# Two-layer attention and FFN kernel: the heads stage's loop over groups written out on four of five engines

## The chip, the cores and the metric

One core of a Trainium2 chip. The core has five engines that run their own instruction streams: TensorE (PE: matmuls, with weight loads shown apart as PEld), VectorE (DVE), ScalarE (ACT), GpSimd (POOL) and SyncE (SP, used here as the queue that issues transfers). They meet only through semaphores. The metric is the device time of one execution in microseconds, lower is better; the time given is the median of the runs.

## What is computed

Two layers, each an attention part and a feed-forward part with a residual, over x of 16 batches x 128 rows x 512 columns. The part that the change touches is the first layer's attention, an mLSTM with 16 heads of 32 columns, whose core is, cut from the reference:

```
log_D = log_fg + transpose(ig)              # gates, lower triangle only
D  = exp(log_D - max_log_D)
C  = einsum('bhsd,bhtd->bhst', qh, kh) / sqrt(dh) * D
normalizer = maximum(abs(C.sum(-1)), exp(-max_log_D))
h  = einsum('bhst,bhtd->bhsd', C / (normalizer + EPS), vh)
hn = (h - mu) * rsqrt(var + EPS) * ln_scale  # per head
x  = x + hn
```

Beside it the same stage computes the keys of the second layer's attention, `ctx @ ki_w + ki_b` (2048 rows x 512 by 512 x 2048), and the sum of their squares, since both read what is already in place.

## The kernel before

The kernel is a row of stages, each with its own block of code for each engine, with a barrier of all engines between stages. The stage of the change is `heads_and_keys`. It works in G = 4 groups of GB = 4 batches. A group has PER = 16 steps; step n stands for head n of the mLSTM and, LAG = 8 steps behind, for head m of the keys. What each engine does in one step:

- PE (L1178, `body`): `keys`, 12 matmuls of 128x512 in three passes (L100 to L102) for one head's keys; in each fourth step (n = 2, 6, 10, 14) `scores` for four heads at once (L1148); then `outputs`, four products of the decayed scores with the values (L1160). `keys` waits for `wt_done` (DVE) and for `ksq_done` of the key two steps earlier (ACT, L944), because the keys use two banks in turn.
- ACT (L950, `body`): in even steps `pair` copies two heads' results out of the bank (L902) and waits for `pv`, the count of PE's `outputs`; then `weight_lead` (L928), `exp` (L892, four calls), `keep_key` (L939, L944, and the transfer L948, which ACT's queue issues). In steps 4 and 5 two squares (L917) and in step 7 a square root (L921) for the group before.
- DVE (L1055): decayed scores (L1008), the weights' low part (L1043), the sum of squares (L1053), and the group before's mean, variance and row statistics.
- POOL (L843): masks (L794), copies of the values (L803), and four element-wise steps for the group before (L779, L820, L830, L839).
- SP (L709): issues all loads, each behind a wait for the buffer that it fills.

Nothing reorders the work: each engine's order is the order of the code above. Group 0 is written out for every engine (`body(0, True)`). Groups 1 to 3 are a hardware loop on each engine: `with act.Fori(1, G) as g` at L971, the same at L1077 (DVE), L864 (POOL) and L1187 (PE), and `sp.Fori(1, G - 1)` at L754, after which SP has its last group written out. In a loop the group number is a register, so that the places and the semaphore values that depend on it are computed by register instructions beside the work. A loop's end is a register add and a conditional branch back to its start; the first instruction behind a taken branch is the register instruction of the same line.

On DVE the helper `Own` counts instructions that wait for their own engine; `enter` and `leave` tell it about the loop.

A later stage, `attend_and_last`, has loops of the same kind for four engines at L2411 and for SP at L2479; the change doesn't touch them.

Of the kernel before, what the change touches and what calls it, by code (L numbers as in the profile page):

```python
# [29 lines left out]
G = B // GB  # L30
# [555 lines left out]
def heads_and_keys(nc, K, M, A, E1, ctx_dram, ln_scale, xn_dram, ct_dram, g_dram, split_dram, w_dram, b_dram, k_dram, rk):  # L586
# [11 lines left out]
    with Phase(nc, "heads") as ph:  # L598
# [72 lines left out]
        def _(sp):  # L671
# [79 lines left out]
            sp.wait_ge(qk, 4)  # L751
            load_q(0, 2)
            body(0, True)
            with sp.Fori(1, G - 1) as g:  # L754
                body(g, False)
            body(G - 1, False, True)
            for m in range(PER - LAG + 1, PER):
# [24 lines left out]
        def _(pool):  # L782
            pool.sem_inc(norm_done, FIRST)
            pool.sem_inc(res_done, FIRST)
            own = Own(pool, own_pool)
# [57 lines left out]
            def body(g, first):  # L843
                for n in range(PER):
                    mask(g, n + AHEAD)
                    if 5 <= n < 8:
                        for b in ((0,), (1, 2), (3,))[n - 5]:
                            value(after(g, PER)[0], g + 1, b)
                    if not first:
                        for at, step in ((3, centre), (8, scale), (10, weigh), (12, add)):  # L850
                            if at <= n < at + 2:
                                step(g - 1, 2 * (n - at))
                                step(g - 1, 2 * (n - at) + 1)
# [7 lines left out]
            nc.gpsimd.memset(total[:], 0.0).then_inc(total_blank, 1)  # L861
            pool.wait_ge(loaded_w, 16)
            body(0, True)
            with pool.Fori(1, G) as g:  # L864
                body(g, False)
            pool.wait_ge(E1.loaded, 48)
            pool.wait_ge(product, (G - 1) * PER)
# [14 lines left out]
        def _(act):  # L882
# [67 lines left out]
            def body(g, first):  # L950
                for n in range(PER):
                    if n % 2 == 0:
                        if n:
                            pair(g, n // 2 - 1)
                        elif not first:
                            pair(g - 1, PAIRS - 1)
                    lagging(g, n - LAG + 1, weight_lead)
                    exp(g, n + 2, first)
                    lagging(g, n - LAG - 1, keep_key)
                    if not first:  # L960
                        if n == 1:
                            row_sums(g - 1)
                        if n == 4 or n == 5:
                            square(g - 1, n - 4)
                        if n == 7:
                            deviation(g - 1)
# [1 line left out]
            exp(0, 0, True)  # L968
            exp(0, 1, True)
            body(0, True)  # L970
            with act.Fori(1, G) as g:  # L971
                body(g, False)
            last = G - 1
            pair(last, PAIRS - 1)
# [25 lines left out]
        def _(dve):  # L1000
            own = Own(dve, own_dve)
# [53 lines left out]
            def body(g, first):  # L1055
                for n in range(PER):
                    decayed(g, n + 1, first)
                    lagging(g, n - LAG + 1, weight_trail)
                    lagging(g, n - LAG - 1, add_square)
                    if not first:  # L1060
                        if n == 1:
                            divisor(g - 1)
                        if n == 1 or n == 2:
                            mean(g - 1, n - 1)
                        if n == 5 or n == 6:
                            variance(g - 1, n - 5)
                        if n == 7:
                            factor(g - 1)
                        if n >= PER - GB // 2:
                            if n == PER - GB // 2:  # L1070
                                dve.wait_ge(res_done, FIRST + g)
                            for b in range(2):
                                row_stats.batch((g - 1) * GB + 2 * (n - PER + GB // 2) + b)

            decayed(0, 0, True)
            body(0, True)
            with dve.Fori(1, G) as g:  # L1077
                own.enter(g - 1, 7)
                body(g, False)
            own.leave(G - 1)  # L1080
            last = G - 1

            def finish(m):
# [1825 lines left out]
```

## Time and profile before

| what | value |
|---|---|
| median of 3 runs | 1503.14 us (1502.87 to 1508.75) |
| the profiled execution, own time | 1506.08 us |
| its span, first to last instruction | 1504.3 us |
| granted TensorE clock, mean over the span | 0.942 of full speed |
| PE busy | 1372.5 us, 91% |
| ACT busy | 771.0 us, 51% |
| DVE busy | 825.4 us, 55% |
| POOL busy | 402.8 us, 27% |
| heads stage, about | 258 to 570 us of the span |

Times in a row are microseconds from the start of the span unless marked ns. A group of instructions has its line, its engine, what it writes and reads, how often it ran, and, in brackets, how long its engine sat idle before it and what it is held to have waited for. An engine's name with a q (ACTq) means its sequencer: register, branch, semaphore and transfer instructions, which don't count as busy. A granted clock of 1.00 means 2.4 GHz, of 0.50 means 1.2 GHz.

### The profile page before, as it was taken

To read this page: it belongs to the slowest core of one execution; us is meant where nothing else is said; L and a number is where in the kernel's file an instruction comes from. 1 tells how busy PE (TensorE), PEld (TensorE's weight loads), DVE (VectorE), ACT (ScalarE), POOL (GpSimd) and SP (SyncE) were. 2 spreads that over 40 slices of the span, in tenths; PEclk is the share of its full clock that TensorE was granted. 3 is DMA by queue.
4 is the path that set the end of the run, shared out by engine and by line. 5 is a ranking of instruction groups with operands and counts; after the bars stand their busy time and mean duration, and the time that the engine had idled before them with its cause. 6 is when DMAs were issued, how large, how long until landed. Compare 5 with 4: busy or idle time off the path is not lost. (4 is left out here: it accounts for less than half of the span.)

```text
span 1504.3 us, 25964 instructions
## 1 busy us (share of the span) xinstructions
PE 1372.5 (91%) x7406; PEld 1138.1 (76%) x7407; DVE 825.4 (55%) x1534; ACT 771.0 (51%) x1874; POOL 402.8 (27%) x375
## 2 busy tenths in 40 slices
PE   6899998999898987998999865999976999999998
PEld 5786666888787867876877644887866888888887
DVE  2432332367676786535444227744328877777866
ACT  4223222578686855215555543535447666666661
POOL 0110101427272810346943015211015500000032
PEclk9999999699999996998999996999987999999999
DMA  7998333887787730347564666654535555555412
GB/s 240 354 337 317 142 140 123 295 285 258 237 267 238 258 115 1 113 154 219 169 195 133 213 226 194 194 200 140 181 112 154 166 157 161 161 159 164 138 48 112
DMA packets 171909, 280.91 MB, mean 187 GB/s; under 512 B 29809, under 2 KB 64369, under 8 KB 171569
## 3 DMA queue, kind: packets, MB, share of 16 engines
q1 hardware_dynamic: 146976, 227.58, 47.6%
q0 software_dynamic: 7712, 26.22, 5.3%
q10 hardware_dynamic: 17136, 26.09, 4.7%
q8 instruction: 40, 0.66, 0.2%
q14 instruction: 45, 0.36, 0.1%
HBM read 173.14 MB, written 106.70 MB: 186 GB/s over the span
## 5 line engine op out<-in xcount | busy, mean ns | idle before, releaser
L2548 ACT ACTIVATE attend_prob<-banks,attend_row,rq 128x128 f32<-128x128 f32 x256 | 113.9, 455 | 53.6 <-DVE attend_row L2623 53.5
L100 PE MATMUL banks<-of_shared_split,heads_wl 128*128 (+1 forms) x256 | 109.6, 428 | 18.6 <-ACT heads_ksq L944 13.5
L100 PE MATMUL banks<-of_shared_split,of_ctx_lead 128*128 128x512 f32 x256 | 106.8, 417 | 9.3 <-DVE of_ctx_trail L419 5.5
L100 PE MATMUL banks<-attend_wol,attend_ol 128*128 (+1 forms) x256 | 105.9, 414 | 0.0
L100 PE MATMUL banks<-of_x_lead,queries_wl 128*128 128x512 f32 x256 | 102.0, 398 | 3.9 <-ACT queries_sq L2183 2.4
L101 PE MATMUL banks<-of_shared_split,heads_wl 128*128 (+1 forms) x256 | 103.8, 405 | 0.0
L102 PE MATMUL banks<-of_shared_split,heads_wt 128*128 (+1 forms) x256 | 103.7, 405 | 0.0
L101 PE MATMUL banks<-of_shared_split,of_ctx_lead 128*128 128x512 f32 x256 | 103.4, 404 | 0.0
L102 PE MATMUL banks<-of_shared_split,of_ctx_trail 128*128 128x512 f32 x256 | 103.2, 403 | 0.0
L101 PE MATMUL banks<-of_x_trail,queries_wl 128*128 128x512 f32 x256 | 101.1, 395 | 0.0
L102 PE MATMUL banks<-of_x_lead,queries_wt 128*128 128x512 f32 x256 | 100.8, 394 | 0.0
L102 PE MATMUL banks<-attend_wol,attend_ot 128*128 (+1 forms) x256 | 100.6, 393 | 0.0
L101 PE MATMUL banks<-attend_wot,attend_ol 128*128 (+1 forms) x256 | 99.7, 389 | 0.0
L2179 ACT ACTIVATE queries_head<-banks,queries_bias 128x512 f32<-128x512 f32 x64 | 44.2, 690 | 95.9 <-PE banks L102 83.8
L1053 DVE TENSOR_TENSOR heads_total<-heads_total,heads_ksq 128x512 f32 (+1 forms) x64 | 62.6, 978 | 53.6 <-ACT heads_ksq L944 53.3
L2255 DVE TENSOR_TENSOR queries_total<-queries_total,queries_sq 128x512 f32<-128x512 f32 x60 | 41.7, 695 | 91.5 <-ACT queries_sq L2183 91.4
L892 ACT ACTIVATE heads_dec<-mlstm_gmax,mlstm_nat 128x128 f32<-128x128 f32 x264 | 83.3, 388 | 5.9 <-POOL mlstm_gmax L794 5.9
L2530 POOL TENSOR_TENSOR x_kept<-x_kept,attend_tern_bias 128x512 f32<-128x512 f32 x12 | 15.5, 1295 | 264.3 <-ACT of_attend_raw L2586 262.7
L2561 ACT ACTIVATE attend_ol<-banks,of_attend_vbias 128x512 fp32r<-128x512 f32 x64 | 44.1, 689 | 70.3 <-PE banks L2753 70.2
L2647 DVE TENSOR_TENSOR x_kept<-x_kept,banks 128x512 f32 (+1 forms) x64 | 44.0, 687 | 62.8 <-PE banks L102 62.2
L1160 PEld LDWEIGHTS banks<-heads_ctx,heads_cmat 128*128 128x128 f32 x512 | 71.6, 209 | 8.6 <-POOL heads_ctx L803 3.1
L2734 PE MATMUL banks<-attend_kn,attend_q 128*128 128x128 f32 x512 | 71.4, 285 | 5.5 <-DMA attend_q<-q_heads 5.5
(339 smaller groups left out, 3612.1 us busy)
## 6 DMA issues: line engine op xcount, KB each, us to landing
mlstm_gmax<-running_max SPq DMA_DIRECT2D x36, 512.0 KB, 5.9
heads_raw<-in_L_xattn_ki_w SPq DMA_DIRECT2D x32, 512.0 KB, 6.3
k_heads<-heads_key ACTq DMA_DIRECT2D x64, 256.0 KB, 4.6
q_heads<-queries_head SPq DMA_DIRECT2D x64, 256.0 KB, 2.4
attend_q<-q_heads SPq DMA_DIRECT2D x64, 256.0 KB, 4.1
of_attend_k<-k_heads SPq DMA_DIRECT2D x60, 256.0 KB, 4.0
of_attend_v<-v_heads SPq DMA_DIRECT2D x60, 256.0 KB, 3.3
sorted_rows<-values_zeros SPq DMA_DIRECT2D x2, 5120.0 KB, 18.1
```

The lines of the kernel that those rows point to most:

```text
L100: nc.tensor.matmul(out, lead_l, lead_r, start=first, stop=False)
L101: nc.tensor.matmul(out, lead_l, trail_r, start=False, stop=False)
L102: return nc.tensor.matmul(out, trail_l, lead_r, start=False, stop=last)
L892: ins = nc.scalar.activation(dec[:, n % 2, b], gmax[:, h // 2 % 4, h % 2 * N + b * S:h % 2 * N + (b + 1) * S], ACT.Exp, scale=-1.0, bias=M ...
L1053: nc.vector.tensor_tensor(t, t, ksq[:, m % 2, :], ALU.add).then_inc(total_done, 1)
L1160: ins = nc.tensor.matmul(ps[:, n // 2 % 2, at:at + DH0 + 1], cmat[:, n % RING, b, :], ctx1[:, bass.ds(half(g), 1), b, n, :].rearrange("p a ...
L2179: nc.scalar.activation(head[:, u % HEADS_RING, :], ps[:, u % 4, :], ACT.Identity, bias=bias[:, h:h + 1]).then_inc(head_done, 1)
L2255: nc.vector.tensor_tensor(t, t, sq[:, u % 2, :], ALU.add).then_inc(total_done, 1)
L2548: ins = nc.scalar.activation(prob[:, j % 2, b, :], ps[:, j % 2, b * S:(b + 1) * S], ACT.Exp, bias=row[:, j % 2, 1, b:b + 1], scale=rq[:, b ...
L2561: nc.scalar.activation(ol[:, par, j, :], ps[:, 4 + j % 2, :], ACT.Identity, bias=vbias[:, bass.ds(quad_of(it) * 4 + j, 1)]).then_inc(ol_do ...
L2647: nc.vector.tensor_tensor(xb, xb, ps[:, 6 + b % 2, :], ALU.add).then_inc(acc_done, 1)
L2734: ins = nc.tensor.matmul(ps[:, j % 2, s], q[:, j, s], kn[:, j % 2, s], start=True, stop=True)
```

## The change

The loops over groups 1 to 3 of ACT, DVE and POOL, and over groups 1 and 2 of SP, become Python loops: the body is written out once for each group, with the group number known when the code is made. PE keeps its hardware loop. `Own` on DVE needs no word about a loop any more.

```
@@ SP, L751 @@
             sp.wait_ge(qk, 4)
             load_q(0, 2)
             body(0, True)
-            with sp.Fori(1, G - 1) as g:
+            for g in range(1, G - 1):
                 body(g, False)
             body(G - 1, False, True)
@@ POOL, L861 @@
             body(0, True)
-            with pool.Fori(1, G) as g:
+            for g in range(1, G):
                 body(g, False)
@@ ACT, L968 @@
             body(0, True)
-            with act.Fori(1, G) as g:
+            for g in range(1, G):
                 body(g, False)
@@ DVE, L1074 @@
             body(0, True)
-            with dve.Fori(1, G) as g:
-                own.enter(g - 1, 7)
+            for g in range(1, G):
                 body(g, False)
-            own.leave(G - 1)
```

Two things follow from the group number being known. The register instructions of these four engines go away. And conditions in the code that ask `isinstance(g, int)` now take the other side; one of them changes a wait (`value`, L797, below).

In the rows that follow, a semaphore that this stage took over from an earlier one stands under its old name: `values_first_loaded0` is `pv`, `values_ct_stored3` and `values_xT_stored` are `raw_loaded`, `values_wt_done` is `product`, `values_x_loaded1` and `values_x_loaded3` are `masked` and `c_done`, `values_product` is `key_done`, `values_cleared` is `total_done`, `values_g_stored` and `values_turned` are `key_stored`. ISA and REGISTER_ALU are register instructions.

ACT, before: the end of step 15 and of the loop's body; behind the branch comes the body's start (L902) again.

```order
L892 ISA
L892 ACTIVATE heads_dec<-mlstm_gmax,mlstm_nat 128x128
L937 ISA [waits values_wt_done]
L939 ACTIVATE heads_key<-banks,heads_kbias 128x512 [waits values_g_stored]
L944 ACTIVATE heads_ksq<-banks,heads_kbias 128x512 [waits values_cleared]
L948 ISA [waits values_product]
L948 DMA k_heads<-heads_key 128x512
L971 REGISTER_ALU
L971 COMPARE_AND_BRANCH
```

ACT, after: the same place, the end of step 15 of group 1 and the start of step 0 of group 2.

```order
L892 ACTIVATE heads_dec<-mlstm_gmax,mlstm_nat 128x128 x3
L939 ACTIVATE heads_key<-banks,heads_kbias 128x512 [waits values_wt_done,values_g_stored]
L944 ACTIVATE heads_ksq<-banks,heads_kbias 128x512 [waits values_cleared]
L948 DMA k_heads<-heads_key 128x512 [waits values_product]
L902 ACTIVATE heads_hraw<-banks 128x4x66 [waits values_first_loaded0]
L928 ACTIVATE heads_wl<-heads_raw 128x512 [waits values_ct_stored3,values_wt_done]
```

The copy of the last pair (L902) now stands directly behind the transfer's issue; the register instruction ahead of each L892, ahead of L939 and ahead of L948 is gone, and no instruction with work in it has another place.

POOL, before: step 5 of the loop's body, where the next group's values are copied; the wait for `pv` stands in each group.

```order
L794 AFFINE_SELECT mlstm_gmax<-mlstm_gmax 128x512 [waits mlstm_g_ring1]
L799 ISA
L801 REGISTER_ALU [waits mlstm_loaded_ctx]
L803 REGISTER_ALU [waits values_first_loaded0]
L803 REGISTER_ALU x2
L803 ISA
```

POOL, after: the same step in group 3, the last.

```order
L794 AFFINE_SELECT mlstm_gmax<-mlstm_gmax 128x512 [waits mlstm_g_ring1]
L803 COPY heads_ctx<-mlstm_ctx 128x16x32 [waits mlstm_loaded_ctx]
L794 AFFINE_SELECT mlstm_gmax<-mlstm_gmax 128x512 [waits mlstm_g_ring1]
L803 COPY heads_ctx<-mlstm_ctx 128x16x32 x2
```

In group 3 the copy for a fifth group (which doesn't exist; the code fills it with group 0's values again) no longer waits for `pv`; in groups 1 and 2 it still does. The order of PE's instructions is the same before and after.

## Rows read from the trace of the kernel before

**Rows 1.** Windows, busy us by engine (count), granted clock, DMA share, GB/s.

```profile
320.07:388.00 67.93, 65.88 (x449) 55.56 (x448) 49.94 (x63) 52.62 (x120) 36.81 (x36) 0.97 0.79 265
388.00:460.31 72.31, 66.14 (x450) 55.75 (x448) 48.90 (x64) 54.67 (x126) 37.86 (x36) 0.95 0.77 249
320.07:323.83 3.76, 3.76 (x22) 3.22 (x20) 1.89 (x3) 3.54 (x9) 0.64 (x1) 1.00 0.99 368
388.00:397.90 9.90, 5.67 (x21) 4.57 (x20) 3.97 (x8) 6.49 (x16) 0.64 (x1) 0.66 0.73 225
460.31:469.64 9.33, 5.40 (x22) 4.36 (x20) 3.60 (x7) 6.49 (x16) 0.64 (x1) 0.82 0.69 227
323.83:329.32 5.49, 5.12 (x54) 4.13 (x52) 4.64 (x9) 4.54 (x11) 0.00 (x0) 1.00 0.79 286
397.90:402.97 5.07, 5.07 (x55) 4.13 (x53) 3.22 (x5) 3.30 (x9) 0.00 (x0) 1.00 0.37 116
353.16:359.69 6.53, 5.28 (x22) 4.26 (x21) 3.95 (x5) 5.25 (x13) 6.53 (x6) 0.75 0.79 277
426.66:431.82 5.16, 3.78 (x22) 3.22 (x21) 3.10 (x4) 5.00 (x13) 5.16 (x5) 1.00 0.82 285
```

**Rows 2.** Waits, 382 to 394: who waited for whom, us in all, times, longest.

```profile
ACT heads_hraw L902 <- PE banks L1160: 6.5, 1, 6.5
DVE heads_wt L1043 <- ACT heads_wl L928: 5.0, 1, 5.0
...
PE banks L100 <- ACT heads_ksq L944: 4.2, 1, 4.2
```

**Rows 3.** Waits, 454 to 466.

```profile
PE banks L100 <- ACT heads_ksq L944: 3.9, 1, 3.9
```

**Rows 4.** Timeline of ACT, 382 to 394: start, us, engine, line, what, [idle before].

```profile
383.27 0.34 ACTq L948 DMA_DIRECT2D k_heads<-heads_key  x1
390.16 0.39 ACT L902 ACTIVATE heads_hraw<-banks 128x264 f32 x1 [6.55 <-PE banks L1160]
```

**Rows 5.** Line L971, 380 to 400: duration ns min/median/max, first and last start.

```profile
L971 ACTq COMPARE_BRANCH  x1: 54/54/54, 383.7 to 383.7; - x1
L971 ACTq FUSED_REGOPS  x1: 59/59/59, 389.8 to 389.8; - x1
```

**Rows 6.** Line L971, 450 to 470.

```profile
L971 ACTq COMPARE_BRANCH  x1: 45/45/45, 455.7 to 455.7; - x1
L971 ACTq FUSED_REGOPS  x1: 59/59/59, 461.8 to 461.8; - x1
```

**Rows 7.** Line L1077 (DVE's loop), 384 to 385.

```profile
L1077 DVEq COMPARE_BRANCH  x1: 63/63/63, 384.2 to 384.2; - x1
L1077 DVEq FUSED_REGOPS  x1: 70/70/70, 384.5 to 384.5; - x1
```

**Rows 8.** Line L1187 (PE's loop), 382 to 383.

```profile
L1187 PEldq COMPARE_BRANCH  x1: 231/231/231, 382.4 to 382.4; - x1
L1187 PEldq FUSED_REGOPS  x1: 59/59/59, 382.7 to 382.7; - x1
```

**Rows 9.** Waits of ACT, 404 to 432.

```profile
ACT heads_wl L928 <- issue: 0.4, 2, 0.3
ACT heads_sq L917 <- POOL heads_hraw L779: 0.2, 1, 0.2
```

**Rows 10.** Waits of POOL, 255 to 560.

```profile
POOL heads_ctx L803 <- PE banks L1160: 7.6, 2, 4.0
```

**Rows 11.** Line L2411 (attend stage's loops), 1248 to 1249.

```profile
L2411 ACTq COMPARE_BRANCH  x1: 45/45/45, 1248.5 to 1248.5; - x1
...
L2411 ACTq FUSED_REGOPS  x1: 59/59/59, 1248.7 to 1248.7; - x1
```

**Rows 12.** Line L2479 (SP's loop there), 1258 to 1260.

```profile
L2479 SPq COMPARE_BRANCH  x1: 50/50/50, 1258.8 to 1258.8; - x1
L2479 SPq FUSED_REGOPS  x1: 73/73/73, 1259.1 to 1259.1; - x1
```

## What is predicted, and from what

> **What bounds the kernel now.** PE is busy 91% of the span, so the first question is where it is not, and the change touches only the heads stage. I read the windows view of that stage first, cut at the starts of PE's `outputs` bursts (L1160), one burst a step. Group 1 takes 67.93 us and group 2, the same work, 72.31 us; PE's busy time in them is 65.88 and 66.14 us [rows 1]. The difference sits in one step: from the burst of step 0 to that of step 1 is 3.76 us in group 1, 9.90 us in group 2 and 9.33 us in group 3 [rows 1]. In the last two the granted clock of that step is 0.66 and 0.82, in the first 1.00: PE fell from 2.4 to 1.2 GHz for a part of the step, right after it had stood idle.
>
> The waits view names who is late. PE's first matmul of step 1 waits 4.2 us for ACT's L944, DVE's L1043 waits 5.0 us for ACT's L928, and ACT's L902 sat idle 6.5 us "for PE's L1160" [rows 2]; in group 3 PE waits 3.9 us at the same place [rows 3]. The last name is wrong. L902 needs `pv` of the burst of step 15, and that burst lies one whole step ahead of the one at 388.0, so it was over some 3 us before. ACT's timeline shows that nothing but a transfer's issue at 383.27 comes before the gap, and L902 starts at 390.16 [rows 4]. What fills the gap is on line L971 itself: the branch back at 383.7, the loop's next register instruction at 389.8 [rows 5], and again 455.7 and 461.8 [rows 6]. That is 6.1 us both times between two instructions of a sequencer that wait for no semaphore. It happens at taken branches only: group 1 is entered from the written-out group 0 with no branch back, and there the step takes 3.76 us.
>
> DVE's branch back costs 0.3 us (384.2 to 384.5) [rows 7] and PE's as much (382.4 to 382.7) [rows 8]. What sets ACT apart is length: between its register instruction at 389.8 and its branch at 455.7 the trace has 390 ACT records; DVE has 148 in its loop, PE 588. So I read the pause as the fetch of the loop's start, no longer held by ACT. The Trainium skill ("Runtime: NRT & Kernel Launch", Instruction fetch mechanics) says that a taken branch whose target is outside the current two-page window forces a fetch before execution goes on; the pause fits that, while the 512 instructions that it gives as ACT's room do not, since 390 would be inside. By the first the pause goes with the branch; by the second it has another cause, which is rival B below.
>
> **The change, part by part.** The sum is made against the profiled execution (1506.08 us, span 1504.3) and carried to the median of the runs, 1503.14, which lies 2.94 us below.
>
> 1. ACT's two taken branches go. With L902 directly behind the transfer's issue, ACT starts step 0 when the burst of step 15 is over, as in group 1, and the step should take 3.76 us. Gain: 9.90 - 3.76 = 6.14 and 9.33 - 3.76 = 5.57 us, 11.71 together; the half-speed time after each pause is in it. What is late next is what is late in group 1 at that point: nothing for the length of one step.
>
> 2. A part comes back. Step 1 to 2 takes 5.49 us in group 1 and 5.07 in group 2 [rows 1]: the pause had let everyone but ACT run ahead. I expect group 1's figure in groups 2 and 3: +0.42 twice, +0.83 with rounding.
>
> 3. ACT's register instructions go. ACT works without a rest from the square at step 4 to step 8, since the square root of step 7 needs two table loads, and the next step of PE waits for it: 5.16 us at clock 1.00 [rows 1] where a step without scores takes about 3.6. In that stretch ACT idles 0.4 us for "issue", twice, and 0.2 us behind POOL [rows 9]. The issue part is its own sequencer: two register instructions and the transfer between one wait and the next. If it all goes, and each step of PE behind it moves up as much, that is 0.4 us a group, 1.2 us for three. Bounds: 0, if the transfer's issue is what fills the gap, and 0.6 x 3 = 1.8. I take 1.2, as most of those instructions are gone.
>
> 4. The branches of DVE, POOL and SP, 0.3 us each: nothing. DVE is covered by its waits for ACT (5.0 us in [rows 2]), POOL and SP run several steps ahead; should that cover go, it is 0.3 us twice, 0.6.
>
> 5. POOL's wait for `pv` in group 3 goes. POOL waited for it 7.6 us in two places [rows 10], and what it copies there nobody reads. POOL comes earlier to its next masks, which wait for transfers anyway. Nothing, and the same if the wait stayed. The order on PE and its loop stay.
>
> 6. The clock. In group 1 the step behind ACT's square root takes 6.53 us at clock 0.75, in group 2 5.16 at 1.00 [rows 1], with nearly the same wait ahead of it. Whether a pause of 1.2 to 1.4 us brings the low clock down on PE seems to be chance: 1.37 us each time. It fell once in three; I count once in three after, so no change, and keep 2 x 1.37 = 2.7 us on the slow side and 1.4 on the fast one.
>
> Sum: -11.71 + 0.83 - 1.2 = -12.1 us, 1503.14 - 12.1 = 1491.1 (1494.0 for the profiled execution). With every bound at its best, -11.71 - 1.8 - 1.4 = -14.9: 1488.2. At its worst, -11.71 + 0.83 + 2.7 = -8.2: 1495.0.
>
> **The rivals.** A, a late fetch in straight code. The written-out groups come through the same transfer engines as the data, whose share is 0.77 to 0.79 here [rows 1]. If one of ACT's pages comes late on the path, the price is that of a pause now, (6.14 + 5.57) / 2 = 5.9 us, and the time 1497.0. Against it: ACT ran group 0 and group 1, one behind the other, without such a pause. The same page of the Trainium skill calls the crossing of a page in straight code mostly hidden; group 1 agrees.
>
> B, the pause is no matter of the branch. If something at the edge of a group holds ACT's sequencer for 6.1 us, it stays, and only part 3 is gained: 1503.14 - 1.2 = 1501.9. For it: 390 instructions are fewer than PE's 588. Against it: group 1's edge has no pause, nor has any other transfer's issue in the stage.
>
> C, slower. The code behind the stage moves in memory, and a later loop that now finds its start in place no longer does. The loop of the attend stage has 131 ACT records and is taken back five times; its branch costs 0.2 us (1248.5 to 1248.7) [rows 11]. If each turn paid the pause, at the 5.9 us that one costs the path here: 5 x 5.9 = 29.5, 1520.6. It decides from the third turn on, 3 x 5.9 = 17.7 against 12.1. Against it: SP's loop with 204 records costs 0.3 us (1258.8 to 1259.1) [rows 12], DVE's with 148 as well, and 131 is less than either.
>
> **How the numbers follow.** The forecast 0.80: the same step without the branch is in the trace. A 0.07, B 0.05, C 0.04, and 0.04 for what I don't see. The predicted time is the forecast's, 1491.1. Its own range, 1488.2 to 1495.0, holds most of the 0.80; to take in the bounds and A the range goes from 1488 to 1497. A measurement of this kernel tells about 0.5% from no change, 7.5 us: under 1495.6 is the forecast whole and part of the unseen, so faster 0.83; A and B are the same, 0.12; C is slower, 0.05 with its share of the unseen.
>
> **What would show it.** In the trace after: no gap of 6 us on ACT at the edges of groups 2 and 3, and step 0 to 1 at 3.8 us with clock 1.00 in all three groups (part 1). Step 1 to 2 at 5.5 us in all three (part 2). The step behind the square root under 5.16 us, and idle "issue" time of ACT below 0.4 us (part 3). PE's wait for L944 in the stage falls from 13.5 to about 5 us. The stages behind keep their lengths; a gap of 6 us on ACT at L2411 would be C, one within a group A. The forecast is wrong if PE, with ACT in time, waits for another engine or a transfer at the same step, so that the step stays over 5 us.

## The result, and the profile after

| | before | after |
|---|---|---|
| median of 15 runs each | 1503.14 us (1500.06 to 1508.83, and one run at 4717.12) | 1493.73 us (1489.45 to 1501.02) |
| the profiled execution, own time | 1506.08 us | 1491.73 us |
| its span | 1504.3 us | 1490.0 us |

The ratio of the runs is 0.9942, with a 95% interval of 0.9925 to 0.9959: 8.7 us less, between 6.2 and 11.3. The median was forecast at 1491.1, in a range of 1488 to 1497. The two profiled executions lie 14.4 us apart, more than the medians do (9.4), and that difference is the second subject of this text.

The waits view of ACT's former edge, 378 to 390 us of the changed kernel, answers [rows 2]: each row is who waited for whom, the time in all, how often, the longest. No row of PE stands in it.

```profile
POOL mlstm_gmax L794 <- DMA mlstm_gmax<-running_max: 11.7, 2, 8.0
DVE heads_total L1053 <- ACT heads_ksq L944: 4.3, 3, 1.6
ACT heads_hraw L902 <- PE banks L1158: 3.0, 2, 2.2
DVE heads_wt L1043 <- ACT heads_wl L928: 0.6, 1, 0.6
```

ACT's wait of 6.5 us is 2.2 us here, and this time the name is right: PE's burst (L1158, the former L1160) is what it waits for. The windows view of the changed kernel, cut at the bursts as in [rows 1], that is at the start of the last matmul ahead of each, 0.2 us before the burst itself (length, busy us of PE, PEld, DVE, ACT, POOL with counts, granted clock, DMA share, GB/s):

```profile
319.51:384.99 65.48, 63.75 (x450) 54.17 (x449) 47.77 (x64) 54.84 (x127) 37.81 (x36) 1.00 0.85 278
384.99:452.11 67.12, 65.42 (x450) 55.37 (x448) 49.27 (x64) 54.54 (x127) 37.17 (x36) 0.97 0.79 266
319.51:323.16 3.65, 3.65 (x22) 3.15 (x21) 1.89 (x3) 3.63 (x9) 0.64 (x1) 1.00 1.04 395
384.99:388.63 3.64, 3.64 (x22) 3.14 (x20) 1.89 (x3) 3.62 (x9) 1.04 (x1) 1.00 0.95 348
452.11:455.76 3.65, 3.65 (x22) 3.15 (x21) 1.89 (x3) 3.35 (x9) 0.64 (x1) 1.00 0.97 343
323.16:328.22 5.06, 5.06 (x55) 4.13 (x53) 4.46 (x8) 4.31 (x11) 0.00 (x0) 1.00 0.83 296
351.82:356.90 5.08, 3.78 (x22) 3.22 (x21) 2.23 (x4) 5.06 (x13) 5.08 (x6) 1.00 0.91 304
417.03:423.43 6.40, 4.82 (x21) 3.93 (x20) 3.74 (x4) 5.57 (x14) 6.40 (x7) 0.82 0.71 261
```

Rows 3 to 5 are the step from burst 0 to burst 1 in groups 1, 2 and 3: 3.65 us with the clock at 2.4 GHz in all three, where groups 2 and 3 had 9.90 and 9.33. The last two are the step behind ACT's square root: PE still stands idle 5.08 - 3.78 = 1.30 us in group 1 and 6.40 - 4.82 = 1.58 us in group 2, and the low clock now falls into group 2. Over the whole stage PE's wait for L944 is 5.1 us, where about 5 were expected and 13.5 stood before.

The stages as wholes, before (the first fence) and after (the second): heads, the stage behind it (`turned_and_shared`), routed experts, queries, attend and last.

```profile
258.13:570.79 312.66, 281.98 (x1856) 238.23 (x1856) 206.06 (x289) 221.74 (x516) 145.51 (x147) 0.91 0.73 239
570.79:670.42 99.63, 94.61 (x467) 81.55 (x468) 50.32 (x146) 33.24 (x58) 33.87 (x38) 0.88 0.27 98
676.40:895.40 219.00, 200.91 (x936) 155.79 (x936) 88.26 (x246) 119.19 (x325) 90.33 (x74) 0.97 0.61 191
895.40:1120.80 225.40, 194.63 (x882) 160.66 (x882) 109.68 (x186) 99.96 (x165) 45.94 (x40) 0.92 0.52 171
1120.80:1504.30 383.50, 363.48 (x2240) 321.07 (x2240) 281.89 (x520) 222.65 (x689) 66.03 (x48) 0.97 0.50 143
```

```profile
257.82:556.60 298.78, 279.34 (x1856) 237.69 (x1856) 201.92 (x289) 221.75 (x516) 144.97 (x147) 0.92 0.75 250
556.60:659.76 103.16, 98.14 (x467) 84.90 (x468) 50.40 (x146) 33.48 (x58) 33.98 (x38) 0.85 0.26 95
665.80:884.00 218.20, 201.90 (x936) 155.84 (x936) 88.24 (x246) 119.40 (x325) 90.36 (x74) 0.96 0.61 192
884.00:1107.30 223.30, 193.08 (x882) 159.57 (x882) 109.39 (x186) 99.96 (x165) 45.47 (x40) 0.93 0.53 172
1107.30:1490.00 382.70, 363.46 (x2240) 321.22 (x2240) 280.67 (x520) 222.43 (x689) 66.57 (x48) 0.97 0.50 144
```

The heads stage is 13.9 us shorter. The stage behind it, whose code the change doesn't touch, is 3.5 us longer, with the same counts on every engine and a lower granted clock, 0.85 against 0.88.

### The profile page after: what moved, and what is told of

Read it like the earlier page. It is cut to its first block and busy times, and to the rows that moved or that the text cites. A ratio compares the mean times of both kernels' runs of the same rounds, so it can differ in the third digit from the quotient of the medians.

```text
span 1490.0 us, 25114 instructions
## 1 busy us (share of the span) xinstructions
PE 1371.7 (92%) x7406; PEld 1139.0 (76%) x7407; DVE 820.2 (55%) x1534; ACT 771.3 (52%) x1874; POOL 402.5 (27%) x375
## 5 line engine op out<-in xcount | busy, mean ns | idle before, releaser
L100 PE MATMUL banks<-of_shared_split,heads_wl 128*128 (+1 forms) x256 | 108.1, 422 | 10.2 <-ACT heads_ksq L944 5.1
L101 PE MATMUL banks<-of_shared_split,heads_wl 128*128 (+1 forms) x256 | 102.2, 399 | 0.0
L1053 DVE TENSOR_TENSOR heads_total<-heads_total,heads_ksq 128x512 f32<-128x512 f32 x64 | 58.8, 919 | 52.4 <-ACT heads_ksq L944 52.2
L892 ACT ACTIVATE heads_dec<-mlstm_gmax,mlstm_nat 128x128 f32<-128x128 f32 x264 | 83.2, 388 | 5.8 <-POOL mlstm_gmax L794 5.8
L1158 PEld LDWEIGHTS banks<-heads_ctx,heads_cmat 128*128 128x128 f32 x512 | 72.0, 210 | 8.7 <-POOL heads_ctx L803 3.1
```

What stands on the lines that cost most here:

```text
L100: nc.tensor.matmul(out, lead_l, lead_r, start=first, stop=False)
L101: nc.tensor.matmul(out, lead_l, trail_r, start=False, stop=False)
L892: ins = nc.scalar.activation(dec[:, n % 2, b], gmax[:, h // 2 % 4, h % 2 * N + b * S:h % 2 * N + (b + 1) * S], ACT.Exp, scale=-1.0, bias=M ...
L1053: nc.vector.tensor_tensor(t, t, ksq[:, m % 2, :], ALU.add).then_inc(total_done, 1)
L1158: ins = nc.tensor.matmul(ps[:, n // 2 % 2, at:at + DH0 + 1], cmat[:, n % RING, b, :], ctx1[:, bass.ds(half(g), 1), b, n, :].rearrange("p a ...
```

## The experiments

Three questions: whether ACT's branch alone does it, whether the pause is the fetch of a loop's start, and why a later stage becomes longer.

### ACT alone, and all but ACT

```
 e1: only ACT's loop            e2: all but ACT's loop
-with act.Fori(1, G) as g:     -with sp.Fori(1, G - 1) as g:   (SP)
+for g in range(1, G):         +for g in range(1, G - 1):
                               -with pool.Fori / dve.Fori(1, G) as g:
                               +for g in range(1, G):
```

> Only ACT's loop over groups is written out; DVE, POOL and SP keep their loops. Theory (the pause at ACT's taken branch is the whole cost): the same as the full change, 1503.1 - 9 to 14 us, no gap of 6 us on ACT, the step from L1160's burst 0 to burst 1 at 3.7 us in all groups. Rival (the register instructions of DVE and POOL carry a part): at least 2 us slower than the full change, seen in the steps 2 and 6, where PE waits for DVE.

> DVE, POOL and SP written out, ACT keeps its loop. Theory: as before the change, 1500 to 1506 us, with two gaps of 6.1 us on ACT at its taken branches and 9 to 10 us for the step behind each. Rival (the gain comes from the engines together): a third or more of the change's gain, 3 us or more.

e1 measured 1495.83 us beside 1502.77 of the kernel before on the same chip, ratio 0.9946 (0.9923 to 0.9969), a gain of 6.9 us between the medians where 9 to 14 were expected; e2 1503.96, ratio 1.0008 (0.9990 to 1.0025). The change itself, on that chip, had 1490.78 us and 0.9930 (e3, below). The step from burst 0 to burst 1 in e1's three groups, by its windows view:

```profile
318.24:321.88 3.64, 3.64 (x21) 3.15 (x20) 1.89 (x3) 3.61 (x9) 0.53 (x1) 1.00 1.05 387
383.77:387.42 3.65, 3.65 (x22) 3.15 (x21) 1.89 (x3) 3.63 (x9) 0.30 (x1) 1.00 0.91 300
451.54:455.19 3.65, 3.65 (x22) 3.15 (x20) 1.98 (x3) 2.75 (x8) 0.00 (x0) 1.00 1.01 308
```

and of e2:

```profile
320.53:324.32 3.79, 3.79 (x22) 3.22 (x20) 1.89 (x3) 3.57 (x9) 0.93 (x1) 1.00 0.96 345
388.73:399.37 10.64, 5.14 (x22) 4.19 (x20) 3.47 (x6) 6.51 (x16) 0.64 (x1) 0.68 0.66 204
462.23:472.39 10.16, 6.05 (x21) 4.86 (x20) 4.41 (x9) 6.51 (x16) 0.64 (x1) 0.71 0.67 212
```

Without ACT's branches nearly the whole gain of the heads stage is there: it takes 300.1 us between its barriers in e1 and 297.0 to 299.8 in three traces of the change, against 312.7 and 313.1 before. With them there is none (315.7 us in e2). The part that the other three engines' loops carry is not told from nothing: e1's median is 5 us above the change's, but the intervals of the two ratios overlap.

That the pause is a fetch can be read from the transfers. The DMA view lists queues that carry instructions. Inside ACT's first pause before (383.8 to 389.7) it has this row (packets, MB, share), and the same one inside the second (455.8 to 461.7):

```profile
q14 instruction: 1, 0.01, 0.3%
```

This one packet of 8 KB starts at 388.19, 4.5 us behind the branch, takes 0.3 us, and ACT's next instruction follows 1.6 us after its start. The ten pauses in the traces of before, e2, e5, e9 and e10 are all alike: one packet, 1.5 to 1.7 us ahead of the end. In e1 and in the change no instruction packet moves between 380 and 390 us. So most of a pause is time before the packet starts, not its own 0.3 us; what the start waits for is open.

### How long a loop may be

Two kernels are the kernel before with empty semaphore increments in the loops' bodies, so that other engines' loops become long too; ACT's is left as it is.

```
 def fill(eng, held, g, count):
     for _ in range(0 if isinstance(g, int) else count):
         ph.hold(eng, held)
+fill(dve, held_dve, g, 7)      # ahead of decayed;          e6: 16
+fill(pool, held_pool, g, 14)   # ahead of mask;             e6: 22
+fill(sp, held_sp, g, 12)       # behind next_raw;           e6: 8
```

> The kernel before, with empty semaphore increments added in the loops' bodies: DVE 7 a step (148 to about 260 instructions in its loop), POOL 14 (96 to about 320), SP 12 (131 to about 323). Theory (an engine's taken branch costs the fetch of the loop's start once the loop is too long to be held): at some length between 204 and 390 the branch back goes from 0.3 to about 6 us on every engine alike; which of the three lengths pays tells the bound. Rival (the 6.1 us belong to ACT alone, to its transfers or its queue): all three stay at 0.3 us.

> The kernel before with more empty increments in the loops: DVE 16 a step (148 to about 404 instructions), POOL 22 (96 to about 450), SP 8 (131 to about 259). In e4 DVE with 260 paid 0.3 us for its branch back, SP with 323 paid 5.3 us, POOL with 322 once 0.3 and once 4.0 us. Theory (a loop of more than some 260 to 320 instructions is fetched anew): DVE and POOL pay 4 to 6 us at every taken branch, SP 0.3 us. Rival (DVE is another kind of engine, or the position in memory decides alone): DVE still at 0.3 us.

Lines L1085, L871 and L760 are here the loops of DVE, POOL and SP. The two ran once each, for their traces (1500.64 and 1502.41 us). e4, the first taken branch of each engine (duration ns, first and last start us):

```profile
L1085 DVEq COMPARE_BRANCH  x1: 63/63/63, 381.0 to 381.0; - x1
L1085 DVEq MOVE  x1: 36/36/36, 381.3 to 381.3; - x1
```

```profile
L871 POOLq COMPARE_BRANCH  x1: 50/50/50, 372.4 to 372.4; - x1
L871 POOLq MOVE  x1: 34/34/34, 378.5 to 378.5; - x1
```

```profile
L760 SPq COMPARE_BRANCH  x1: 53/53/53, 381.6 to 381.6; - x1
L760 SPq FUSED_REGOPS  x1: 55/55/55, 386.9 to 386.9; - x1
```

e6, DVE and SP:

```profile
L1085 DVEq COMPARE_BRANCH  x1: 63/63/63, 380.7 to 380.7; - x1
L1085 DVEq MOVE  x1: 36/36/36, 386.0 to 386.0; - x1
```

```profile
L760 SPq COMPARE_BRANCH  x1: 53/53/53, 381.6 to 381.6; - x1
L760 SPq FUSED_REGOPS  x1: 55/55/55, 382.0 to 382.0; - x1
```

Taken branches by the number of records between two branches of a loop; all loops of these traces that are left out have at most 204 records, or are PE's, and cost 0.2 to 0.4 us:

| records in the loop | engine, kernel | branch to the loop's first instruction |
|---|---|---|
| 96 to 148 | POOL, SP, DVE, before | 0.3 to 0.4 us |
| 204 | SP, attend stage, before | 0.3 us |
| 259, 260 | SP in e6, DVE in e4 | 0.3 to 0.4 us |
| 322, 323 | POOL, SP in e4 | 6.1 and 4.0; 5.3 us |
| 390 | ACT, in all seven traces with its loop | 5.2 to 7.1 us |
| 404, 448 | DVE, POOL in e6 | 5.3 and 6.3; 5.5 and 5.1 us |
| 588 | PE, all | 0.3 us |

The pause belongs to no engine in particular, and between 260 and 322 records it sets in; PE alone goes back over 588 without one. There is a second instruction queue, q8, with packets of 16 KB. It moves five from 300 to 390 us and none from 390 to 553, while PE goes through groups 2 and 3, as PE's would if PE held its loop; that q8 is PE's, the profile doesn't say. From 390 to 553 the view has only this row of instructions:

```profile
q14 instruction: 10, 0.08, 0.1%
```

(The expectation of e6 gives POOL's branches in e4 as 0.3 and 4.0 us; the 0.3 was the start of a mask that had been queued before the branch, and the register instruction came after 6.1 us.) The Trainium skill ("Runtime: NRT & Kernel Launch", Instruction fetch mechanics) gives such a stall for a branch out of the window that is held, with 512 instructions of room for most engines and 2048 for PE. The stall and the larger room of PE agree with these traces; 512, read as a length that any loop may have, does not, since 322 already pays. The pages are said to come in blocks of 256 instructions in 16 KB; on q14 this case's packets have 8 KB (45 of them, 0.36 MB), on q8 16 KB (40, 0.66 MB). Length is not parted from place here: each length stands at one place in the code, a loop of 322 can touch three blocks of 256 where one of 260 may touch two, and no run moved a loop without changing its length. So 260 and 322 are lengths that went well and badly, not a bound for every kernel.

One more thing is read here. At the first edge of e4 ACT's pause (380.5 to 386.3) and SP's (381.6 to 386.9) overlap, at both edges of e6 ACT's (380.2 to 385.4 at the first) and DVE's (380.7 to 386.0); POOL, steps ahead, has ended its own about 2 us or more before. The step behind takes 9.0 to 10.2 us in these two traces, against 8.6 to 10.8 where only ACT pauses. Pauses that overlap don't add.

### Once more the same kernels: where the rest of the gain goes

> The changed kernel once more, beside the others on one chip, for its scatter. Theory (the median gains less than the one trace, 9.4 against 14.4 us, because low-clock stretches of PE after short waits come and go from run to run): the steps of the heads stage are again 3.7 us behind step 0 in all groups, and the trace differs from the last one only where the granted clock differs. Rival (a stage behind the heads stage has become longer in most runs): a later stage is longer than before at the same clock.

> The kernel before once more, for a second trace of the stage behind the heads stage, which took 99.6 us before and 103.2, 105.1 and 107.9 us in the traces of the change, of e3 and of e1, with 31 us at the low clock before and 41 to 51 us there. Theory (that stage's low clock is chance, and only this one trace of before was lucky): 103 us or more here. Rival (the change makes that stage longer): 99 to 100 us again.

> The changed kernel a third time, beside e8 on one chip. Heads stage between its barriers again 299 us (311.8 before). Theory (scatter of the low clock in the stage behind): that stage anywhere from 99 to 108 us. Rival (the change makes it longer): 103 us or more again.

e3: 1490.78 us, ratio 0.9930 (0.9903 to 0.9958). e7: 1491.24, ratio 0.9947 (0.9923 to 0.9971). e5, the kernel before (one run, 1504.58 us), has the next stage at 99.5 us again, so the theory written for it (one lucky trace) is wrong: the traces of the kernel before agree, and those of the change don't have that length. But neither was "the change makes it longer" yet an answer, since e11, below, has a written-out ACT and 99.4 us. The windows view of the stage in six more traces, cut at its barriers, one fence each, in this order: before again (e5), the change (e3, e7), then kernels of the next two sections (e9, e10, e11).

```profile
569.88:669.41 99.53, 94.51 (x467) 81.48 (x468) 50.28 (x146) 33.21 (x58) 33.84 (x38) 0.88 0.27 98
```

```profile
556.17:661.33 105.16, 100.63 (x467) 87.12 (x468) 50.33 (x146) 33.59 (x58) 34.13 (x38) 0.82 0.26 93
```

```profile
551.21:658.89 107.68, 103.69 (x467) 90.60 (x468) 50.58 (x146) 33.54 (x58) 33.92 (x38) 0.80 0.25 91
```

```profile
568.97:674.30 105.33, 100.54 (x467) 87.12 (x468) 50.37 (x146) 33.57 (x58) 33.97 (x38) 0.82 0.26 93
```

```profile
572.43:679.61 107.18, 103.17 (x467) 90.27 (x468) 50.49 (x146) 33.68 (x58) 33.91 (x38) 0.80 0.25 91
```

```profile
550.58:649.95 99.37, 94.37 (x467) 81.41 (x468) 50.38 (x146) 33.22 (x58) 33.99 (x38) 0.88 0.28 98
```

Counts are the same in all of them and the busy times of DVE, ACT and POOL within 0.5 us; length and granted clock move together. The stage begins at 1.2 GHz with PE nearly idle (busy 1.1 of the first 5 us in the kernel before), and the clock rises and falls again in its first 48 us: in the trace of before it is low to 578.35, from 588.59 to 595.41 and from 598.83 to 609.07, in e9's to 575.87 and in one piece from 582.69 to 613.41. Between 400 and 700 us all changes of the granted clock in a trace lie on one even raster. What goes with the stage's length is where it starts against that raster. Take this place in the first trace as 0, later starts as positive:

| place | kernels | next stage, of it at 1.2 GHz |
|---|---|---|
| -0.5 to -0.4 us | e2, change, e8 | 103.0 to 103.2 us, 32 us |
| 0 to 0.5 us | before, e5, e4, e6, e11 | 99.4 to 99.6 us, 24 to 25 us |
| 0.7 to 0.9 us | e9, e12, e3 | 105.2 to 105.3 us, 37 to 38 us |
| 1.0 us | e1, e7 | 107.7 to 107.8 us, 44 us |
| 2.1 us | e10 | 107.2 us, 43 us |

Fourteen traces, and each group has one length to 0.3 us, whatever the kernel is. The starts can be checked against the last fall of the clock before them: they lie 6.1 to 6.6 us behind it in the second row, 6.8 to 7.0 in the third, 7.1 in the fourth and 8.2 in the last; in the first row 5.7 (e8) or, where that fall came one edge of the raster earlier, 9.0 to 9.1 (e2, the change). The change alone stands in three rows (103.2, 105.2 and 107.7 us), and e8 and e11, one kernel too, in two (103.0 and 99.4), so the code doesn't decide the length. The table was made after ten of these traces; e9 to e12 were then run to test it.

### Moving the place on purpose

```
             dve.wait_ge(rk_done, 1)
             own(nc.vector.reciprocal(rk[:], rk[:]))
+            for _ in range(10):          # e9; e10: 25; e12, on e8: 5
+                dve.sem_inc(own_dve, 1)
```

> The kernel before with 10 empty semaphore increments at the very end of DVE's part of the heads stage, ahead of the barrier: the next stage starts about 0.9 us later, and nothing else changes. In ten traces that stage's length went with where the heads stage ended against the edges at which the granted clock changes: four traces that agree to 0.4 us gave 99.5 us with 24 us at the low clock, ends about 0.7 us earlier 103.1 us with 32, ends 0.7 to 0.9 us later (or as much as a whole period of the records away from it) 105 to 108 us with 37 to 44. Theory (the end's place against those edges decides): 105 to 108 us for the next stage, with 37 to 44 us at the low clock, and a time of some 6 to 9 us over the kernel before. Rival (something in the written-out code makes that stage longer): 99.5 us again and a time 1 us over the kernel before.

> The same with 25 increments, about 2.3 us. Theory: another length of the next stage than 99.5 us, between 103 and 108, since the end now lies between the places where 105 to 108 and 103 were seen. Rival: 99.5 us, and 2.3 us in all.

The ten increments take 0.95 us on DVE, but PE leaves the barrier only 0.6 us later than it would have: 1.56 us behind the start of DVE's last reciprocal, where the kernel before has 0.93. In e10 it is 2.0 us later. e9's trace has the next stage at 105.33 us and e10's at 107.18 us, against 99.5 in the four traces of loops on ACT that end at the usual place: 0.6 us of delay in the heads stage makes the next stage 5.8 us longer. So the theory of the place stands, and the rival, something in the written-out code, falls. In the medians there is less of it. e9: 1505.18 us beside 1503.45, ratio 1.0013 (0.9986 to 1.0040), under the 6 to 9 us that were expected; e10: 1510.33 us, ratio 1.0036 (1.0011 to 1.0060). A part may come back in the queries stage, which takes 224.4 us in e9 from barrier to barrier on PE, against 226.1 before. For the rest it is open: timed runs leave no trace, only a mean clock, and 23 runs of the kernel before on this chip lie from 1498.3 to 1515.0 us, so its place too must move from run to run, if the traces' reason holds there.

### A version that beats both

PE's wait of 1.3 to 1.6 us behind the square root had not gone. The timeline shows why. ACT in group 2 of the changed kernel:

```profile
412.76 1.28 ACT L921 ACT_TABLE_LOAD   x1
414.06 0.35 ACT L921 ACTIVATE heads_small<-heads_small,eps 128x64 f32<-128x64 f32 x1
415.01 0.39 ACT L902 ACTIVATE heads_hraw<-banks 128x264 f32<-128x264 f32 x1 [0.60 <-PE banks L1158]
415.29 0.63 ACT L928 ACTIVATE heads_wl<-heads_raw 128x512 fp32r<-128x512 f32 x1
415.94 1.28 ACT L892 ACT_TABLE_LOAD   x1
417.23 1.28 ACT L892 ACTIVATE heads_dec<-mlstm_gmax,mlstm_nat 128x128 f32<-128x128 f32 x4
418.42 0.67 ACT L939 ACTIVATE heads_key<-banks,heads_kbias 128x512 f32<-128x512 f32 x1
418.99 0.67 ACT L944 ACTIVATE heads_ksq<-banks,heads_kbias 128x512 f32<-128x512 f32 x1
```

and PE beside it:

```profile
413.63 0.97 PE L1158 MATMUL banks<-heads_ctx,heads_cmat 128*128 x8
417.25 0.97 PE L1158 MATMUL banks<-heads_ctx,heads_cmat 128*128 x8
419.80 0.47 PE L100 MATMUL banks<-of_shared_split,heads_wl 128*128 x1 [1.58 <-ACT heads_ksq L944]
```

ACT is done with the square root at 414.41 and idles 0.60 us until the burst of 413.63 is over. From there L902, L928, a table load, `exp` and `keep_key` follow, and PE goes on at 419.80. Being earlier at L921 would only lengthen the 0.60 us. So e8 changes the order: in steps 5 to 9 `keep_key` goes ahead of `exp`, whose result DVE needs a step later.

```
+key_first = not first and 5 <= n <= 9
+if key_first:
+    lagging(g, n - LAG - 1, keep_key)
 exp(g, n + 2, first)
-lagging(g, n - LAG - 1, keep_key)
+if not key_first:
+    lagging(g, n - LAG - 1, keep_key)
```

> On top of the change: in steps 5 to 9 of groups 1 to 3 ACT does keep_key (L939, L944) ahead of exp (L892). Theory (PE's wait of 1.3 to 1.6 us behind the square root is a chain from one step's outputs over pair, weight_lead, a table load of 1.28 us, exp of 1.28 us and keep_key, so that register instructions could not shorten it): the table load and exp leave the chain, the wait and the one of 0.4 us at step 6 go, and with them low-clock stretches of 1.3 us: 4 to 6 us less than the change, step 8 to 9 at 3.6 us. Rival (ACT is short of throughput there): the wait comes back one or two steps later, gain under 2 us.

e8: 1484.16 us beside 1502.05 before and 1491.24 of the change (e7) on the same chip, 7.1 us less than the change where 4 to 6 were expected; ratio to before 0.9894 (0.9857 to 0.9931). The step behind the square root:

```profile
412.20:415.85 3.65, 3.65 (x22) 3.15 (x21) 2.90 (x4) 3.62 (x9) 3.65 (x4) 1.00 0.99 333
```

3.65 us where it was 6.40, all of it with PE at work at 2.4 GHz; it is 3.65 us in all three groups. The smaller wait at step 5 to 6 went too: 4.86 us in each group, where the change's first trace had 5.2 to 5.6. The heads stage takes 292.3 us, against 297.0 to 299.8 in the traces of the change. The wait doesn't come back later, so ACT was not short of throughput there.

> The kernel of e8 once more, to be compared with e12 on one chip: 16 to 19 us under the kernel before, the stage behind at 103 us or more.

> The kernel of e8 with 5 empty increments, about 0.5 us, at the end of DVE's heads stage. Theory: the next stage falls from 103 to 99.5 us in the trace, and the median is up to 3 us under that of e11, less where the heads stage's own scatter of half a microsecond moves the end out of the good place. Rival: 0.5 us slower than e11.

e11: 1484.89 us, ratio 0.9862 (0.9822 to 0.9903). e12: 1486.69 us, ratio 0.9870 (0.9830 to 0.9909). e12 missed: 105.26 us for the next stage where 99.5 were expected, and a median 1.8 us above e11's, not under it. Its five increments moved the barrier by 0.1 us, not by 0.5, and e11, the same kernel without them, had this time ended at the good place by itself (99.37 us). The places of e8 and e11 lie 0.9 us apart, so a fixed delay can't steer a place that moves by so much between executions of one kernel. e12's own trace stands in the table's third row, as its place says, but it is no test of a delay. e8 and e11, one kernel, are the fastest of this study, 18 to 19 us under the kernel before by the medians.

## Right and wrong, by the prediction's own steps

**The reading of the pause** was right: ACT's own taken branch, not PE, held L902 (e1, e2), the instruction packet stands inside the pause, and other engines pay the same once their loops are long (e4, e6). The length at which a loop becomes too long was not in the trace of before, which, PE apart, had only 204 and 390.

**Part 1**, 11.71 us: 9.90 - 3.64 = 6.26 and 9.33 - 3.65 = 5.68, together 11.94 us. Right.

**Part 2**, 0.83 us coming back: wrong. Step 1 to 2 takes 5.06 us in group 1, not 5.49. In group 2 nothing came back (5.06 us) and in group 3 0.1 us, while group 1 gained 0.4. From the first matmul of burst 1 to that of burst 2 group 1 takes 5.27 us before, 4.92 in e1, 4.94 in e2 and 4.83 in the change, so a part of the 5.49 was a cost of register instructions, on ACT and on the others, and went with them.

**Part 3**, 1.2 us at the square root: wrong in place. The step went from 5.16 to 5.08 us, 0.1 instead of 0.4 us a group, since ACT waits for PE inside the chain that I took for a throughput limit. The idle "issue" time did go, as said. What register instructions gave, they gave in part 2 and in small pieces: to the last burst, 528.03 before and 514.23 after by the same marks, the trace gains 13.8 us, of which part 1 is 11.9 and 0.3 lie ahead of the heads stage.

**Parts 4 and 5**, nothing: e2 shows nothing for the loops of DVE, POOL and SP. POOL's wait in group 3 is gone in e2 as well, but wasn't tried apart.

**Part 6**, the clock behind the square root: one low stretch in three groups before, one after in the first trace and in e7, two in e3 and in e1. Its price was a little low: 6.40 - 5.08 = 1.3 us in the step itself, but with what reaches into the next step 1.6 to 1.9 us in the traces of e1 and the change. Nor is it chance which group has it: in before, e2, e5, e9 and e10 it is group 1 each time and no other, in e1 and the change never group 1.

**"The stages behind keep their lengths"** is the step that was wrong. Over the traces of the same two kernels the heads stage goes from 312.7 and 313.1 to 298.8, 299.8 and 297.0 us, 14.4 less in the mean; the next stage from 99.6 and 99.5 to 103.2, 105.2 and 107.7, 5.8 more. These two leave 8.6, but that this is the 8.7 of the ratio is chance: the spans of the same five traces lie 14.7 us apart in the mean, since from barrier to barrier 2.7 us less go to the queries stage, 1.8 to the attend stage, 0.3 to the experts, and 1.4 to what lies ahead of the heads stage, where the change can't act.

So why the timed runs gain less (9.4, 12.0 and 10.8 us between medians, on three chips) is only known in part. Each run's span and mean granted clock are on record, and an estimate of its time at 1.2 GHz follows from them: 161 and 163 us in the mean for 23 and 17 runs of the kernel before, on the chips of e3 and e7; 168, 161 and 163 us for the 15, 6 and 12 runs of the change. The five traces have 175 and 165 before, 167, 149 and 152 after. In the traces the change has less low clock, in the timed runs it has no less; in which stage they have it is open.

The forecast of 12.1 us lies between the 14.4 of the profiled executions and the 9.4 of the medians. That it is near both is in part luck: the heads stage gained more than was added up (13.9 us), and the stages behind, put at nothing, moved by several us either way.

**The rivals.** A, a late fetch in straight code: in groups 1 to 3 every gap of over 1.5 us on ACT in the traces of the change ends with a burst of PE. Behind the last group L928 has one of 5.2 us with no releaser named (528.59 to 533.77), but no instruction packet stands in it, and the kernel before has the same one (4.9 us). B, a pause that stays: no. C, a later loop that pays: the attend stage took 383.5 us before and 382.7 after, and ACT's branches in it cost 0.3 us. None of them is what took the gain.

## What to carry to other kernels

When an engine idles "for" another at the top of a loop, look at the sequencer's rows of the loop's own line: if the branch and the next register instruction are microseconds apart, no wait stands between and an instruction packet does, the loop is too long for that engine, and here only that engine's loop had to be written out. Before you cost a queue's shorter instructions as a gain, follow the chain back one more step and see whether the queue waits for its consumer inside it. And a time saved in a stage that hands over to one with a low and changing clock is not saved yet: compare the next stages' length and clock in more than one trace.

## What the hardware showed that I had not expected

- On DVE and SP a loop of 260 instructions goes back in 0.3 to 0.4 us, on POOL and SP one of 322 in 4.0 to 6.1 us, about as ACT's of 390 does; on PE 588 go back in 0.3 us.
- Of ACT's pause of 5.4 to 7.1 us 3.9 to 5.5 pass before its one instruction packet of 8 KB starts (ten pauses in five traces).
- A delay of 0.6 us ahead of a stage made that stage 5.8 us longer, with 38 in place of 24 us of it at 1.2 GHz, and the same code had one of a few lengths, 99.5, 103.1, 105.3 or 107.7 us, by where it started against the moments at which the granted clock changed.
